# One fused audio-tower kernel on one core: the same instructions in another order on all five engines, and another assignment of PSUM banks

## The reference

```python
h = frames @ dct.T                                   # 938 x 128
y = attn(layernorm(h)); h = h + y                    # linear attention with decay, 4 heads of 32
z = ffn(layernorm(h));  h = h + z                    # expert b % 8 of 8
# attn(x):
n = ln1(x);  xx = n shifted by one frame
q, k, v = (n*tm + xx*(1-tm)) @ W.T  for tm_q, tm_k, tm_v;  g = sigmoid((...tm_g) @ Wg.T)
q = exp(rmsnorm(q)); k = exp(rmsnorm(k))
A_t = lam * A_{t-1} + k_t v_t^T ; z_t = lam * z_{t-1} + k_t
x = x + (g * (q_t A_t) / (q_t z_t)) @ Wo.T
x = x + gelu(ln2(x) @ W1.T) @ W2.T                   # 128 -> 512 -> 128
# ffn(x):
xa = ln(x) @ attn_w.T + attn_b + x
h1 = gelu(xa @ fc1[e].T + fc1_b[e]);  out = gelu((h1 @ fc2[e].T + fc2_b[e]) @ next_w.T + next_b)
```

## Time and profile before

| | us |
|---|---|
| median of 3 runs | 1168.7 |
| lowest and highest | 1149.69 and 1169.6 |
| profiled execution | 1150.52 |
| its span, first to last instruction | 1148.7 |
| mean granted TensorE clock | 0.966 |

### The profile page before, as it was taken

The page is one execution under the profiler, slowest core; times in us unless marked ns, Lnnn a source line. Parts: engine busy times, 40 slices in busy tenths (PEclk is TensorE's granted clock), DMA queues, the critical chain, the costliest instruction groups (busy, mean ns, idle before and its releaser), DMA issues.

```text
span 1148.7 us, 48873 instructions
## 1 busy us (share of the span) xinstructions
PE 1012.2 (88%) x20963; PEld 769.8 (67%) x20963; DVE 922.8 (80%) x2690; ACT 662.5 (58%) x1240; POOL 368.8 (32%) x175
## 2 busy tenths in 40 slices
PE   6669898998989989899999989988897979989887
PEld 6557576776667657586776767667675766757664
DVE  6889788896887968789898888878798876888742
ACT  3237574755746557475656757555575736757454
POOL 4323134241332513225142322414233251322311
PEclk9789999999999999999999999999999989999999
DMA  5423323142330413204142331414233141321320
GB/s 175 149 65 101 89 53 105 42 131 67 90 99 18 136 56 107 81 22 138 50 125 74 107 90 36 123 41 125 74 106 82 27 125 58 107 74 38 105 67 18
DMA packets 71638, 97.06 MB, mean 84 GB/s; under 512 B 11360, under 2 KB 46720, under 8 KB 71424
## 3 DMA queue, kind: packets, MB, share of 16 engines
q1 hardware_dynamic: 71424, 93.94, 28.4%
HBM read 27.89 MB, written 10.83 MB: 34 GB/s over the span
## 4 chain that ended last, share of the span: by engine, by line
PE 62%; issue 17%; DVE 15%; POOL 4%; DMA 1%; ACT 1%; SPq 0%; DVEq 0%; POOLq 0%
PE bank L1025 10%; PE bank L1191 9%; PE bank L1197 8%; PE bank L1030 6%; PE bank L1162 5%; PE bank L1169 5%; PE bank L1107 5%; DVE qq L776 3%; POOL rr L459 2%; PE bank L1102 2%; PE bank L1139 2%; PE bank L1146 2%; DVE st L702 2%; PE bank L1185 2%; POOL rr L450 1%
## 5 line engine op out<-in xcount | busy, mean ns | idle before, releaser
L1107 PE MATMUL bank<-qx,ki 128*32 128x16 f32 x7680 | 132.9, 193 | 30.2 <-issue 30.2
L438 POOL TENSOR_TENSOR nrm<-ssq,phalf 128x8 f32<-128x8 f32 x32 | 52.4, 1637 | 300.4 <-DVE ssq L752 300.3
L610 ACT ACTIVATE hid<-bank,f1b 128x512 f32<-128x512 f32 (+1 forms) x128 | 81.5, 648 | 102.3 <-PE bank L1191 97.8
L1107 PEld LDWEIGHTS bank<-qx,ki 128*32 128x32 f32 x7680 | 116.1, 112 | 32.4 <-issue 32.3
L459 POOL TENSOR_TENSOR rr<-vv,nhalf 128x8 f32<-128x8 f32 x32 | 78.5, 2452 | 158.2 <-DVE vv L715 158.2
L1169 PE MATMUL bank<-w,hid 128*128 128x128 f32 x1024 | 125.2, 281 | 2.7 <-ACT hid L590 1.5
L1191 PE MATMUL bank<-xa,f1w 128*128 128x512 f32 (+1 forms) x256 | 122.6, 616 | 4.0 <-issue 4.0
L565 ACT ACTIVATE px<-bank 128x256 f32<-128x256 f32 (+1 forms) x128 | 48.2, 377 | 132.8 <-PE bank L1146 104.4
L1169 PEld LDWEIGHTS bank<-w,hid 128*128 128x128 f32 x1024 | 120.3, 196 | 5.2 <-ACT hid L590 2.9
L444 POOL TENSOR_TENSOR ab<-af,heads 128x1792 f32<-128x1792 f32 x16 | 94.0, 5876 | 67.7 <-DVE af L815 67.7
L1162 PE MATMUL bank<-c,w 128*128 128x512 f32 (+1 forms) x256 | 113.9, 568 | 0.9 <-ACT c L584 0.9
(11 more groups left out here) (143 smaller groups left out, 2434.7 us busy)
## 6 DMA issues: line engine op xcount, KB each, us to landing
qx<-qq SPq DMA_DIRECT2D x256, 80.0 KB, 2.1
hs<-hs SPq DMA_DIRECT2D x32, 532.0 KB, 4.2
zq<-rz_dram SPq DMA_DIRECT2D x64, 128.0 KB, 4.7
gz<-gate_f SPq DMA_DIRECT2D x16, 512.0 KB
xT<-in_xT SPq DMA_DIRECT2D x16, 468.5 KB, 3.0
v_a<-v_f SPq DMA_DIRECT2D x16, 256.0 KB
v_b<-v_f SPq DMA_DIRECT2D x16, 256.0 KB
f1w<-in_fc1T SPq DMA_DIRECT2D x16, 256.0 KB
```

The source lines that it names most:

```text
L1107: return mm(D[r, :, t + j:t + WIN:EIGHT], ki[:, j, s0:s0 + WIN], x[:, :, t0 + j:t0 + WIN:EIGHT], start=True, stop=True)
```

## The change: the order of the steps, and the banks

No instruction is added or taken out; every step is issued for the same samples. Four things move. On TensorE the 32-wide steps stand among the wide ones in smaller groups. On VectorE the steps around the block states (`chain`, which feeds `states` on GpSimd) and the rms norms stand in another order. On ScalarE, GpSimd and SyncE the steps follow. `USES` has the banks for the new order. Some steps are also written under the next `at(n)`, because they now stand on the other side of a round's end.

```diff
 USES = [
-    [("qT0", 2), ("v1", 2), ("g1", 2), ("w1_12", 3), ("w2_1", 3), ("f1_00", 3), ("nmT1", 3), ("at1", 3), ("f1_13", 3), ("q1", 1)],
...
+    [("w1_01", 3), ("v0", 2), ("n2T1", 3), ("w1_13", 3), ("n1T0", 3), ("f1_00", 3), ("f1_03", 3), ("n1T1", 3), ("wo0", 2), ("f2_1", 3), ("qT0", 1)],
...
 @block.sync
                 if (b := at(2)) is not None:
-                    hand_h1(b)
-                if (b := at(3)) is not None:
-                    expert(b)
-                if (b := at(2)) is not None:
-                    spread(b, 1); hand_h2(b)
+                    hand_v(b); hand_h1(b); spread(b, 1); rz_out(b); rz_back(b); hand_h2(b); spread(b, 2); spread(b, 3)
+                    hand_gate(b)
...
+                if (b := at(2)) is not None:
+                    expert(b)
+                if (b := at(1)) is not None:
+                    spread(b, 0)
 @block.gpsimd
-                if (b := at(1)) is not None:
-                    powq(b, 1)
-                if (b := at(2)) is not None:
-                    pow2(b, 0)
-                if (b := at(1)) is not None:
-                    powq(b, 0)
-                if (b := at(2)) is not None:
-                    resid(b, 0); pow2(b, 1); pow3(b, 0); resid(b, 1)
+                if (b := at(2)) is not None:
+                    resid(b, 0); pow2(b, 0)
+                if (b := at(1)) is not None:
+                    powq(b, 0); powq(b, 1)
+                if (b := at(2)) is not None:
+                    resid(b, 1); pow2(b, 1); pow3(b, 0)
                 if (b := at(1)) is not None:
                     states(b)
 @block.vector
...
                 if (b := at(2)) is not None:
-                    zmul(b); chain(b); from_start(b)
+                    denominators(b); from_start(b); chain(b)
...
-                    qlev(b, 1)
...
+                    zscan(b); decayed(b); zmul(b); qlev(b, 1)
...
 @block.tensor
...
-                    pairs(b, 2); zts(b); scan(b, 0); pairs(b, 3); scan(b, 1)
-                if (b := at(3)) is not None:
-                    f1s(b, 0, 0); f1s(b, 0, 1); f1s(b, 0, 2); f1s(b, 0, 3); n1Ts(b, 1); nmTs(b, 1); f2s(b, 0)
...
+                    pairs(b, 2)
+                if (b := at(3)) is not None:
+                    f1s(b, 0, 0); f1s(b, 0, 1); f1s(b, 0, 2)
+                if (b := at(2)) is not None:
+                    pairs(b, 3); scan(b, 0)
+                if (b := at(3)) is not None:
+                    f1s(b, 0, 3); f2s(b, 0); nmTs(b, 1)
+                if (b := at(2)) is not None:
+                    scan(b, 1); scan(b, 2)
...
-                    pairs(b, 6); pairs(b, 7); scan(b, 4); scan(b, 5)
...
+                    pairs(b, 6)
                 if (b := at(3)) is not None:
                     f2s(b, 1)
                 if (b := at(2)) is not None:
-                    n2Ts(b, 0); scan(b, 6); scan(b, 7)
+                    n2Ts(b, 0); scan(b, 4); scan(b, 5); pairs(b, 7)
+                if (b := at(1)) is not None:
+                    qkTs(b, 0, 0); qkTs(b, 1, 0)
                 if (b := at(3)) is not None:
                     oTs(b, 1)
                 if (b := at(2)) is not None:
-                    w1s(b, 0, 0)
+                    w1s(b, 0, 0); scan(b, 6); scan(b, 7)
```

More of the change, by code:

```diff
@@ L618, in body @@
             def body(at):
+                if (b := at(3)) is not None:
+                    gelu1(b, 0, 1); gelu1(b, 0, 2); gelu1(b, 0, 3)
                 if (b := at(2)) is not None:
-                    gelu1(b, 0, 2); gelu1(b, 0, 3)
+                    tanhs(b, 0); vcopy(b, 0)
+                if (b := at(3)) is not None:
+                    normed2(b, 1)
+                if (b := at(2)) is not None:
+                    exps(b, 1, 1); vcopy(b, 1)
+                if (b := at(3)) is not None:
+                    c1s(b, 1)
@@ L621, in body @@
+                if (b := at(2)) is not None:
+                    pxs(b, 0); exps(b, 0, 1); tanhs(b, 1)
+                if (b := at(3)) is not None:
+                    gelu1(b, 1, 0); gelu1(b, 1, 1); gelu1(b, 1, 2); gelu1(b, 1, 3); n2s(b, 0)
                 if (b := at(1)) is not None:
-                    exps(b, 0, 0); exps(b, 1, 0); vcopy(b, 0); exps(b, 0, 1)
+                    hcopy(b, 0)
                 if (b := at(2)) is not None:
-                    normed2(b, 1)
+                    pxs(b, 1)
@@ L625, in body @@
+                if (b := at(3)) is not None:
+                    xas(b, 0); nms(b, 0)
                 if (b := at(1)) is not None:
-                    vcopy(b, 1)
+                    hcopy(b, 1)
+                if (b := at(3)) is not None:
+                    gelu2(b, 0, 0); gelu2(b, 0, 1); gelu2(b, 0, 2)
                 if (b := at(2)) is not None:
-                    c1s(b, 1)
-                if (b := at(1)) is not None:
-                    tanhs(b, 0); tanhs(b, 1); exps(b, 1, 1)
+                    pxs(b, 2)
@@ L631, in body @@
+                if (b := at(3)) is not None:
+                    gelu2(b, 0, 3); n2s(b, 1); nms(b, 1)
+                if (b := at(2)) is not None:
+                    pxs(b, 3)
+                if (b := at(1)) is not None:
+                    hlT(b, 0)
+                if (b := at(3)) is not None:
+                    xas(b, 1); fin(b, 0)
+                if (b := at(1)) is not None:
+                    hlT(b, 1)
                 if (b := at(2)) is not None:
-                    gelu1(b, 1, 0); gelu1(b, 1, 1); gelu1(b, 1, 2); gelu1(b, 1, 3); n2s(b, 0)
@@ L670, in body @@
-                if (b := at(1)) is not None:
-                    gelu1(b, 0, 0); gelu1(b, 0, 1)
+                    gelu1(b, 0, 0)
             every_round(body)
@@ L917, in body @@
                     merge(b, 0)
-                if (b := at(3)) is not None:
-                    hidden(b, 1)
-                if (b := at(2)) is not None:
-                    qlev(b, 1)
-                if (b := at(3)) is not None:
-                    stats3(b, 1)
-                if (b := at(2)) is not None:
-                    merge(b, 1)
                 if (b := at(1)) is not None:
@@ L928, in body @@
                 if (b := at(2)) is not None:
-                    denominators(b)
+                    merge(b, 1)
                 if (b := at(3)) is not None:
-                    x_attn(b, 0)
+                    hidden(b, 1); x_attn(b, 0); stats3(b, 1)
                 if (b := at(1)) is not None:
                     variance1(b)
+                if (b := at(2)) is not None:
+                    gate(b, 0); gate(b, 1)
                 if (b := at(3)) is not None:
@@ L940, in body @@
                 if (b := at(2)) is not None:
-                    between(b, 1); gate(b, 0); gate(b, 1); merge(b, 3)
+                    between(b, 1); merge(b, 3)
                 if (b := at(3)) is not None:
@@ L1250, in body @@
                 if (b := at(2)) is not None:
-                    pairs(b, 4); scan(b, 2); scan(b, 3); pairs(b, 5)
+                    scan(b, 3); pairs(b, 4)
                 if (b := at(3)) is not None:
-                    oTs(b, 0); f1s(b, 1, 0); f1s(b, 1, 1); f1s(b, 1, 2)
+                    oTs(b, 0); f1s(b, 1, 0); f1s(b, 1, 1)
+                if (b := at(2)) is not None:
+                    attends(b, 0); pairs(b, 5)
+                if (b := at(3)) is not None:
+                    f1s(b, 1, 2)
                 if (b := at(1)) is not None:
-                    qkv(b, "k", 0); qkv(b, "k", 1)
+                    qkv(b, "q", 0)
                 if (b := at(3)) is not None:
```

140 lines of the change are left out of this document (47 added, 93 removed), and 8 rows, old and new, of the table USES.

## The result

The changed kernel took 1055.95 us, the median of 4 runs (1051.41 to 1058.2). The kernel before took 1165.26 beside it. The ratio is 0.9131, with a 95% interval of 0.9035 to 0.9228. The profiled executions span 1054.6 us after and 1148.7 before.

A forecast was written before the change was run, and what follows sets the result against it. TensorE was taken as the bound, stopping for pieces of its instruction list. From 1150.5 us, - 75 - 13 - 15 + 15 + 22 + 2 = -64 gave 1086; a count by rounds gave 1068; 1075 was taken between, range 1045 to 1105 (0.67).

The forecast's parts named there:

- the second count: One full-clock TensorE round without its stops, plus switches, stops left and waits: 62.9 us instead of 68.6, giving 1068 us.
- The stops: TensorE in 32-wide runs: instructions arrive in pieces of 256, short pieces wait; mixing gains 75 us, range 60 to 88.
- The count of short pieces: Pieces of TensorE's list with under 3.7 us of work: 76 lacking 115 us before, 27 lacking 21 after.
- rival of contention: Other DMAs set the piece spacing, so stops stay at other places: 1135 to 1150 us, chance 0.05.
- The clock: TensorE's clock stays up without long stops ahead of wide products: 13 us gained, bounds 5 and 22.
- Low stretches only in the first 80 us: Sign looked for on TensorE: no low-clock stretches later than that, granted clock above 0.98.
- VectorE beside GpSimd: qlev beside states delays merges that pair products wait for; all 15 us of these waits go, bounds 0 and 15.
- More changes between wide and 32-wide: TensorE: four more groups in each of 16 rounds, 0.23 us each for going in and out: +15 us.
- The second rival: Slower: a TensorE stop is the price of a 32-wide group, not of a piece: 1185 us, chance 0.04.
- New waits: Tight handoffs between engines in the new order cost 1.4 us a round: +22 us, from 5 to 56.
- seven tight handoffs: Handoffs with under half a microsecond to spare in a round of some 60 us; only the first below zero, by 0.3.
- The end and the start: Only the end was priced: in the last round nms and ats(b, 1) are no longer hidden by nmTs(b, 1), +2 us.

The follow-up runs named there:

- grouped: Changed kernel with the 32-wide groups put together again on TensorE alone, other engines as changed: 1200.06 us, 1.0317 of the kernel before.
- the control: The changed kernel itself, unchanged, run again as yardstick beside the follow-up runs: 1057.4 us, 0.9113 of the kernel before.
- mixed alone: Kernel before with wide products moved between the 32-wide groups on TensorE alone, banks and other engines' orders as before: 1209.17 us, 1.0425.

## Why the prediction was right

The predicted 1075 us is 1.8% above the median of 1056. The main cause is the one that it gave: the stops have the largest share of the gain, and grouping again brings them back. That the size came out so near is in part luck. The sum of the terms gave 1086, 30 us too slow, and only the mean with the second count (1068) brought it to 1075. In the terms of that second count, a round was to hold 0.8 us of stops and 1.4 of waits; measured over the 13 rounds it holds (21.0 + 20 x 0.2) / 13 = 1.9 of stops and no waits. The two errors nearly cancel: 59.8 + 0.9 + 1.9 = 62.6, against 62.5 measured and 62.9 forecast. By its steps:

- **The stops.** Gain 63 us where 75 stood; what stays in the `issue` rows of 32-wide lines is 26 us (14.4 + 7.6 + 1.9 + 1.6), not below 20. The count of short pieces (76 to 27) had the right course; the size was off: I took one spacing of 3.7 us. The runs show two. Among stops with the DMA engines nearly idle (share under 0.1) the median distance between two pieces is 3.7 us before the change; with a share over 0.9 it is 5.0 in the changed kernel, since the packet starts 2.6 us after the piece ahead and not 1.1. So a piece with 3.8 us of own work, full by my count, still stopped in `us`. My rival of contention was right about what is left: the earlier trace rows had a 4.06 us piece with a DMA share of 0.56, which I took only as the upper end of one spacing. With the copies out of the way stops are at 19, about the 16 forecast.
- **The clock.** 9 us by the table, some 15 to 18 by the stretches at half clock, where 13 stood; the mean granted clock went from 0.966 to 0.986. One reason given for 1.0 us a stretch does not hold, that 32-wide work doesn't slow: in the low stretches of the kernel before, a state product (L1139) took 25 ns from start to start in the mean and 14.5 outside them, an in-block one (L1107) 15.5 and 11.3. "Low stretches only in the first 80 us" failed once: a stop of 3.22 us ended at 737.09, and 1.5 us of work later TensorE ran at 0.50 (1.2 GHz), in this stretch of 3.4 us:

```profile
738.60:742.00 3.40, 3.40 (x11) 0.87 (x13) 0.00 (x0) 1.39 (x3) 1.40 (x1) 0.50 0.02 5
```

- **VectorE beside GpSimd.** The waits for merges fell from 15.8 to 0.8 us, as forecast, and `qlev` takes 1.01 us (594.63 in VectorE's timeline) where the earlier trace rows had 4.11. What was incomplete is to count only the merges as waiting behind `qlev`. Put back in the new order, it costs 32 us, and `x_attn` is as late as the merges are; in the old one, taking it away gave about 10 us where 15 stood. The prediction also saw only `qlev`: `nb` and `nrm` beside `resid` gave VectorE another 30 us, and what these are worth was not tried apart.
- **More changes between wide and 32-wide.** +12 us, forecast +15. Read from both traces, going in costs 0.09 us and coming out 0.11 to 0.13. The Trainium skill (TensorEngine Tiling, Key Properties) says that a change of tiling mode drains the engine; the traces agree with a cost at each change, and these are the prices. It is not what the stops were: `grouped`, with 77 groups less, was 13% slower than the control and not faster. The second rival is out.
- **New waits.** This was the step that failed: +22 us were forecast, and none came. Of the seven tight handoffs none shows in the 13 full rounds. TensorE's waits from 117.44 to 930.56, whole; all 20 end where a piece of the list begins, so they are stops:

```profile
PE bank L1058 <- issue: 11.9, 11, 2.4
PE bank L1086 <- issue: 6.7, 6, 3.2
PE bank L1004 <- issue: 2.1, 2, 1.4
PE bank L1125 <- issue: 0.3, 1, 0.3
```

  I had laid the work out in a round of 60 us; at 62.5 each handoff has more room, and the first, which I put 0.3 below zero, had it too. The waits fell by 33 us over the span, 15 of them those for merges. The experiments show that the risk was real: `mixed alone` and `grouped` have 120 and 88 us of such waits, and one moved step of VectorE brings them to 57. That the longer round is what gave the handoffs their room is argued, not shown; which of the many moved steps of the other engines does it I have not taken apart, but for `qlev`.
- **The end and the start.** Behind the 13 rounds it got 5 us shorter, where I had +2; ahead of them 10 us shorter, which I had not priced apart.

What I looked for in the profile held for the round (62.5, forecast 62 to 64), the clock and `qlev`; it failed for the `issue` rows (26, forecast below 20) and for "no distance below 3.5 us": 7 pieces after, and 23 before, began less than 3.5 us after the one ahead (1.8 us at the least). For three of the 7 the packet had started before the piece ahead began; the other four had it 0.9 to 1.2 us behind that, and began 2.2 to 2.4 us later. What asks for a packet, and so when it may be early, stays open.

## What to carry to other kernels

An engine that stops with no partner in the profile, in dense runs of small instructions, may be short of instructions: count its list, look whether the stops come at one place modulo a fixed number, and mix long instructions in till each piece has more work than a piece takes to arrive. Then look at what else is in the DMA queues when such a piece is due: a large copy that nobody waits for belongs beside the long instructions. And a new order of one engine is worth its price only with the orders of the others: here the new orders without the mixing lost 3%, a mixing without them lost 4%, and both together gained 9%.

## What the hardware showed that I had not expected

- The instructions of an engine are DMA packets of 16 KB in a queue of their own, and other transfers delay them: packet start 1.06 us after the piece ahead began with the DMA engines idle (28 stops of the kernel before), 2.56 us with them busy over 0.9 (32 stops in three traces of the changed kernel). The packet's own time is little changed (1.0 to 1.1 us in the median of each trace, 1.9 at most but for one of 2.3), so it is late in starting, not slow. From its start to the first product of the piece that stopped it is 2.4 to 2.7 us in the median of each trace.
- A VectorE instruction of 0.42 us that comes while GpSimd's `states` runs doesn't slow down by some factor: it ends 0.3 us after GpSimd does. Where `states` took 5.25 us, the two instructions of `qlev` took 5.70 together, of which 1.1 is their own; the one that had begun before `states` was not touched. Instructions of 0.17 us were held the same way: `nb` and `nrm` beside `resid` (L455) before, 15 times each, and `vv` beside `states` in the kernel before with `qlev` moved, 13 times. `nrm` and `vv` have one input.
- In the view of waits, `issue` also covers waits for VectorE's semaphore that the profile doesn't resolve (52.8 us in 16 waits of `mixed alone`).
